# ScalarE and GpSimd preparing the next sub-block, and a transpose moved between two products, in a two-layer kernel's solve stage

## The reference, cut to what matters

```
logits = einsum('bhqd,bhkd->bhqk', q, k) * scale
probs = softmax(logits + causal_mask)
L = eye(s) - tril(probs, -1)
rhs = diagonal(probs)[..., None] * v
A = solve_triangular(L, rhs, lower=True)          # s = 512 rows, one after the other
attn_output @ Wd.T + bd
...
h = gelu(einsum('ecd,edf->ecf', exp_batches, c_fc))
exp_out = einsum('ecf,efd->ecd', h, c_proj)
```

## Time and profile before

| | |
|---|---|
| median of 3 runs | 1405.09 us (1400.81 to 1409.5) |
| the profiled execution's own time | 1403.81 us |
| its span, first to last instruction | 1401.9 us |
| busy in the span: PE, PEld, DVE, ACT, POOL | 981.4, 766.5, 900.0, 466.1, 341.8 us |
| mean granted TensorE clock | 0.818 of full |
| the four `solve_block` stages | about 595 to 713, 808 to 924, 1040 to 1157, 1241 to 1358 us of the span |

### The profile page before, as it was taken

The page is one execution under the profiler, slowest core; times in us unless marked ns, Lnnn a source line. Parts: engine busy times, 40 slices in busy tenths (PEclk is TensorE's granted clock), DMA queues, the critical chain, the costliest instruction groups (busy, mean ns, idle before and its releaser), DMA issues. The chain is left out here.

```text
span 1401.9 us, 29590 instructions
## 1 busy us (share of the span) xinstructions
PE 981.4 (70%) x10762; PEld 766.5 (55%) x10762; DVE 900.0 (64%) x3559; ACT 466.1 (33%) x1066; POOL 341.8 (24%) x390
## 2 busy tenths in 40 slices
PE   5376599970665056877769968769986777986754
PEld 5165499960621034666545657646665655775643
DVE  5656262216789065888768888758878970058857
ACT  1233244424224003311235411235532126941215
POOL 1277154540047170021210021210001230012221
PEclk9788799995579587966889966789977788987877
DMA  9397598836018864410034220044411005411008
GB/s 220 46 209 210 155 249 238 228 95 180 26 50 237 244 151 123 113 28 20 21 97 129 77 61 20 22 110 125 114 46 36 24 21 163 136 45 38 28 22 235
DMA packets 241824, 153.95 MB, mean 110 GB/s; under 512 B 80432, under 2 KB 226096, under 8 KB 241424
## 3 DMA queue, kind: packets, MB, share of 16 engines
q1 hardware_dynamic: 232528, 133.04, 37.0%
q0 software_dynamic: 9152, 19.02, 4.2%
HBM read 96.76 MB, written 55.24 MB: 108 GB/s over the span
## 5 line engine op out<-in xcount | busy, mean ns | idle before, releaser
L1157 DVE TENSOR_REDUCE mx<-banks 128x1 f32<-128x384 f32 (+3 forms) x352 | 203.3, 634 | 72.6 <-PE banks L1088 72.0
L1323 DVE TENSOR_TENSOR prod<-A,Kst_Pn 128x8 f32<-128x8 f32 (+30 forms) x992 | 179.4, 221 | 0.6
L1329 DVE TENSOR_REDUCE A<-prod 128x4 f32<-128x8 f32 (+30 forms) x992 | 174.8, 217 | 0.0
L800 POOL DMA_INDIRECT o_dram<-step_o,step_to x80 | 81.4, 1017 | 309.4 <-ACT step_o L789 297.2
L1137 ACT ACTIVATE Eoff<-banks 128x256 f32<-128x256 f32 (+2 forms) x192 | 114.9, 598 | 102.6 <-PE banks L1073 93.6
L1071 PE MATMUL banks<-Qexp,Kst_Pn 128*128 128x256 bf16 x640 | 115.5, 282 | 44.1 <-DMA Qmax<-q_stack 34.0
L1139 ACT ACTIVATE Ed<-banks 128x256 f32<-128x256 f32 x256 | 98.0, 383 | 111.4 <-PE banks L1073 111.4
L1084 PE MATMUL banks<-masks,identb 128*128 128x128 bf16 (+2 forms) x352 | 90.3, 256 | 59.8 <-DMA Qmax<-q_stack 50.9
L1088 PE MATMUL banks<-Kst_Pn,Qmax 128*128 128x128 bf16 (+3 forms) x512 | 123.3, 313 | 0.0
L756 PE MATMUL banks<-step_xT,step_w 128*128 128x256 f32 x320 | 105.8, 488 | 22.5 <-issue 22.0
L1263 POOL TENSOR_TENSOR A<-A,Kst_Pn 128x256 f32<-128x256 f32 x16 | 19.4, 1213 | 408.0 <-DVE Kst_Pn L1293 408.0
(11 more groups left out here) (197 smaller groups left out, 1816.0 us busy)
## 6 DMA issues: line engine op xcount, KB each, us to landing
Kst_Pn<-k_stack SPq DMA_DIRECT2D x32, 512.0 KB, 4.6
rows_dram<-blank SPq DMA_DIRECT2D x12, 858.0 KB, 12.1
e_w<-in_L_w1T_dram SPq DMA_DIRECT2D x39, 256.0 KB
e_w<-in_L_w2T_dram SPq DMA_DIRECT2D x39, 256.0 KB
Qmax<-q_stack SPq DMA_DIRECT2D x64, 96.0 KB
Qexp<-q_stack SPq DMA_DIRECT2D x64, 96.0 KB
Kst_Pn<-k_stack SPq DMA_DIRECT2D x16, 384.0 KB, 4.5
step_xt<-rows_dram SPq DMA_DIRECT2D x40, 132.0 KB, 2.2
```

The costliest lines, as they stand in the source:

```text
L800: self.nc.gpsimd.indirect_dma_start(self.o_dram, bass.IndirectOffsetOnAxis(self.to[n][:, j:j + 1], 0), self.o[n][:, j, :], None).then_inc( ...
L1157: nc.vector.tensor_reduce(out, logits, AX_X, ALU.max, negate=True).then_inc(max_done, 1)
L1323: nc.vector.tensor_tensor(prod[:, ds, 0:r + 1], A[:, ds, k0:k0 + r + 1], Pn[:, c * SUB + r:c * SUB + r + 1, 0:r + 1].broadcast_to([P, HD / ...
L1329: nc.vector.tensor_reduce(A[:, ds, k0 + r], prod[:, ds, 0:r + 1], AX_X, ALU.add).then_inc(row_done, 1)
```

## The change

VectorE now multiplies only the first sub-block's probabilities. For sub-blocks 1 to 3 ScalarE copies the turned probabilities from PSUM into `Pn` as they are (`keep_probs`), and GpSimd, one sub-block ahead, forms the first term, multiplies `Pn` by `rZ`, multiplies `A` by the diagonal, sets the diagonal to 1 and adds the term (`prepare`). `turn_before(c+1)` moves ahead of sub-block c's recurrence, so that for sub-block 1 it stands before the first recurrence of the block. TensorE's transposes of the next expert tile move between a tile's `up` and its `down`, and ScalarE's copy of them behind the tile's second gelu.

```diff
                 for g in range(per_sub * c, per_sub * (c + 1)):
-                    if g >= 2:
-                        pe.wait_ge(probs_in, g - 1)
+                    if g < 2 * per_sub:
+                        pe.wait_ge(probs_in, g - per_sub + 1)
+                    else:
+                        pe.wait_ge(probs_kept, g - 2 * per_sub + 1)
                     turn_probs(nc, Ed, ident, bank[g % 2], g).then_inc(probs_turned, 1)
...
                 for k in tiles[c]:
-                    steps.turn(pe, k)
+                    if k == tiles[0].start:
+                        steps.turn(pe, k)
                     steps.up(pe, k)
+                    if k + 1 < tiles[-1].stop:
+                        steps.turn(pe, k + 1)
                     steps.down(pe, k)
...
         def _(act):
+            def keep_probs(c):
+                for g in range(per_sub * c, per_sub * (c + 1)):
+                    act.wait_ge(probs_turned, g)
+                    nc.scalar.copy(Pn[:, g * TURN:(g + 1) * TURN, :],
+                                   bank[g % 2][:, 0:TURN * SUB].rearrange("p (q k) -> p q k", k=SUB)).then_inc(probs_kept, 1)
+
             for c in range(NSUB):
+                if c + 1 < NSUB:
+                    keep_probs(c + 1)
                 for k in tiles[c]:
-                    steps.keep_turned(act, k)
+                    if k == tiles[0].start:
+                        steps.keep_turned(act, k)
                     steps.gelu(act, k)
+                    if k + 1 < tiles[-1].stop:
+                        steps.keep_turned(act, k + 1)
                     steps.keep_out(act, k)
...
         def _(pool):
+            own = Chain(pool, own_done)
...
+            def own_term(c):
+                ts = slice(t0 + c * SUB, t0 + (c + 1) * SUB)
+                own(nc.gpsimd.tensor_tensor(A[:, :, ts], A[:, :, ts],
+                                            diagonal(c).rearrange("p (a i) -> p a i", a=1).broadcast_to([P, HD, SUB]), ALU.mult))
+                own(nc.gpsimd.memset(diagonal(c), 1.0))
+
+            def prepare(c):
+                qs, ts = slice(c * SUB, (c + 1) * SUB), slice(t0 + c * SUB, t0 + (c + 1) * SUB)
+                z = rZ[:, qs].rearrange("p (q a) -> p q a", a=1)
+                pool.wait_ge(z_done, c)
+                own(nc.gpsimd.tensor_tensor(term[:, :, :], before[:, :, 0:HD].rearrange("p q d -> p d q"),
+                                            rZ[:, qs].rearrange("p (a q) -> p a q", a=1).broadcast_to([P, HD, SUB]), ALU.mult))
+                pool.wait_ge(probs_kept, per_sub * c)
+                own(nc.gpsimd.tensor_tensor(Pn[:, qs, :], Pn[:, qs, :], z.broadcast_to([P, SUB, SUB]), ALU.mult))
+                own_term(c)
+                own(nc.gpsimd.tensor_tensor(A[:, :, ts], A[:, :, ts], term[:, :, :], ALU.add))
+
+            pool.wait_ge(probs_in, per_sub)
+            own_term(0)
             for c in range(NSUB):
...
+                if c + 1 < NSUB:
+                    prepare(c + 1)
                 for k in tiles[c]:
                     steps.send(pool, k)
...
+            turn_before(0)
+            first_terms()
+            turn_before(1)
             for c in range(NSUB):
-                turn_before(c)
                 if c:
                     keep_rows(c - 1)
-                add_before(c)
-                if c:
+                    if c + 1 < NSUB:
+                        dve.wait_ge(own_done, 2 + 5 * c)
+                        turn_before(c + 1)
                     add_later(c)
-                dve.wait_ge(own_done, 2 * c + 2)
```

More of the change, by code:

```diff
@@ L1191, in solve_block @@
         sb, sem = tensors(nc, ctx)
-        own_done, base_done = sem("own_done"), sem("base_done")
+        own_done, base_done, probs_kept, z_done = sem("own_done"), sem("base_done"), sem("probs_kept"), sem("z_done")
         probs_turned, probs_in = sem("probs_turned"), sem("probs_in")
@@ L1257, in _, with diagonal @@
         def _(pool):
-            for c in range(NSUB):
[L1259 to L1266, removed]
+            own = Chain(pool, own_done)
+            def diagonal(c):
+                first = c * SUB * SUB
+                return Pn.rearrange("p q k -> p (q k)")[:, first:first + (SUB - 1) * (SUB + 1) + 1:SUB + 1]
+            def own_term(c):
[15 more added lines that the diff above has]
+            own_term(0)
+            for c in range(NSUB):
+                if c + 1 < NSUB:
+                    prepare(c + 1)
                 for k in tiles[c]:
@@ L1274, in _, with add_term, first_terms @@
             base = Chain(dve, base_done)
-            def add_term(c, sums):
+            def add_term(c, sums, out, ready):
                 qs = slice(c * SUB, (c + 1) * SUB)
                 ts = slice(t0 + c * SUB, t0 + (c + 1) * SUB)
[L1279 to L1282, removed]
+                base(nc.vector.tensor_tensor(out, sums, rZ[:, qs].rearrange("p (a q) -> p a q", a=1).broadcast_to([P, HD, SUB]), ALU.mult))
+                dve.wait_ge(own_done, ready)
+                base(nc.vector.tensor_tensor(A[:, :, ts], A[:, :, ts], out, ALU.add))
             def turn_before(c):
                 base(nc.vector.transpose(before[:, :, :], RT[:, c, :, :].rearrange("p t q -> p q t")))
-                base(nc.vector.reciprocal(rZ[:, c * SUB:(c + 1) * SUB], before[:, :, HD]))
-            def add_before(c):
-                for g in range(per_sub * c, per_sub * (c + 1)):
+                if c:
+                    nc.vector.reciprocal(rZ[:, c * SUB:(c + 1) * SUB], before[:, :, HD]).then_inc(z_done, 1)
+                else:
+                    base(nc.vector.reciprocal(rZ[:, 0:SUB], before[:, :, HD]))
+            def first_terms():
+                for g in range(per_sub):
                     gs = slice(g * TURN, (g + 1) * TURN)
@@ L1295, in add_before @@
                                             ALU.mult).then_inc(probs_in, 1)
-                add_term(c, before[:, :, 0:HD].rearrange("p q d -> p d q"))
+                add_term(0, before[:, :, 0:HD].rearrange("p q d -> p d q"), later[:, :, :], 2)
             def keep_rows(c):
@@ L1305, in add_later @@
                 base(nc.vector.transpose(later[:, :, :], wide[:, 0:SUB * HD].rearrange("p (t d) -> p d t", d=HD)))
-                add_term(c, later[:, :, :])
+                dve.wait_ge(z_done, c)
+                add_term(c, later[:, :, :], later[:, :, :], 2 + 5 * c)
+            turn_before(0)
+            first_terms()
+            turn_before(1)
             for c in range(NSUB):
-                turn_before(c)
                 if c:
                     keep_rows(c - 1)
-                add_before(c)
-                if c:
+                    if c + 1 < NSUB:
+                        dve.wait_ge(own_done, 2 + 5 * c)
+                        turn_before(c + 1)
                     add_later(c)
-                dve.wait_ge(own_done, 2 * c + 2)
                 k0 = t0 + c * SUB
```

## The result

The changed kernel takes 1414.94 us, the median of 11 runs (1410.99 to 1417.96); the kernel before, over 11 runs in all, 1405.09 (1399.17 to 1409.5). The ratio is 1.0072 with a 95% interval of 1.0055 to 1.0088: slower by 0.7%. The forecast was 1414. The profiled execution took 1415.38, its span 1413.5, which is 11.6 longer than before.

What follows compares the result with a forecast made beforehand. VectorE was taken to set nine of 16 sub-block stretches, TensorE seven. Terms -8.8 + 10.0 + 12.7 + 11.2 - 2.6 - 6.0 - 3.15 - 3.0 gave +10.3 on 1403.81, or 1414 us; range 1385 to 1430.

Steps and rivals of the forecast that it cites:

- block's start: Before each block's first recurrence: the turning for sub-block 1 and a memset wait cost 2.5 a block, +10.0 us.
- lock: GpSimd's SBUF reads hold VectorE's recurrence multiplications: +12.7 us in sub-block 0, +11.2 in sub-block 1; also counted in sub-block 2.
- tiles: Expert tiles: hidden transposes take 1.0 a tile off TensorE's path; sub-block 2 -2.6 and -6.0 us, sub-block 3 -3.15.
- crossings into 1 and 2: From turn_rows to later_sums: the row copy no longer waits behind turning sums, 1.1 at eight crossings, -8.8 us.
- block's end: Earlier GpSimd sends let VectorE's last copy close three of four blocks, 1.0 each, -3.0 us.
- GpSimd beside the recurrence: GpSimd and VectorE take exclusive turns at SBUF: each small operation costs VectorE 0.38 us, the 128x1024 one 2.03.
- second rival: In the recurrence, GpSimd holds VectorE for the whole instruction, 0.69 and 2.76 us: +20.7, 1424 us; chance 0.17.
- first rival: In the recurrence, GpSimd gives way and VectorE doesn't lose: -17.0, 1387 us; chance 0.18.
- third rival: In the tiles, the moved transposes aren't hidden and TensorE's stretches stay as long: +25.1, 1429 us; chance 0.06.
- the 16 stretches: Sub-block spans from later_sums to turn_rows before the change: TensorE taken to set seven, VectorE nine.

Runs made afterwards that it cites:

- e6: Changed kernel with GpSimd's four reading operations per prepared sub-block replaced by memsets that read nothing: 1381.31 us, ratio 0.9844.
- e1: Kernel before with only the expert-tile transposes moved between up and down, and ScalarE's copy behind the gelu: 1379.81 us, ratio 0.9817.
- e10: Changed kernel with useless transposes filling TensorE's waits before turn_rows in sub-blocks 0, 1 and 3, three per recurrence row: 1406.80 us, ratio 1.0001.
- e2: Changed kernel with only the moved transposes taken back, ahead of each tile: 1433.41 us, ratio 1.0201.
- e5: Kernel before with the transposes moved and, at a crossing, the copy of rows ahead of turning the sums: 1375.38 us, ratio 0.9792.
- e8: e5 with useless transposes, four each behind a few late recurrence rows of sub-blocks 0, 1 and 3: 1363.35 us, ratio 0.9702.

## Why the prediction was right, and where two terms were wrong

By its own steps, in us over the four blocks, measured as after less before from the table:

| term | predicted | measured |
|---|---|---|
| sub-block 0 (block's start 10.0 and lock 12.7) | +22.7 | +22.7 |
| sub-block 1 (lock) | +11.2 | +9.4 |
| sub-block 2 (tiles, lock) | -8.6 | -10.0 |
| sub-block 3 (tiles) | -3.15 | -3.2 |
| crossings into 1 and 2 | -8.8 | -1.8 |
| block's end | -3.0 | -7.6 |
| not forecast: `later_sums` +1.7, crossing into 3 -0.1, elsewhere +0.5 | 0 | +2.1 |
| sum | +10.3 | +11.6 |

*GpSimd beside the recurrence* was the step on which the sign hung, and it held: e6 takes the loss away and leaves the rest. The multiplications grew by 34.3 where 35 was forecast. The split was off in both parts and the errors cancelled: a big operation costs 1.40 to 1.63, not 2.03; a small one 0.53, not 0.38. Three guesses were behind that. The big operation takes 1.91 whole, so its hold was not four times the small one's 0.55. VectorE is let go only a little before GpSimd ends: the held pair ends at 642.02 + 1.83 = 643.85 and needs its usual 0.32, so the hold ended near 643.53, 0.13 before GpSimd's 643.66. That is the 0.14 of the last stage's copy (0.61 - 0.47), and it did not grow with the operation. And what VectorE can do meanwhile isn't half a pair of reductions but the whole pair: GpSimd gets in as a pair of multiplications ends (641.75 beside 641.54 + 0.32), and the reductions stand next. So the second rival had the better mechanism, nearly the whole instruction, with a price that no row bore out (2.76). The first rival, that VectorE doesn't lose, would have brought sub-blocks 1 to 19.3; they took 21.72.

*The block's start* came out to the tenth. Timeline of VectorE after, against the earlier trace rows:

```profile
604.20 0.43 DVE L1316 TENSOR_TENSOR A<-A,later 128x256 f32<-128x256 f32 x1 [1.09 <-POOL Kst_Pn L1284]
604.66 2.01 DVE L1319 STREAM_TRANSPOSE before<-RT 128x1024 f32<-128x1024 f32 x1
...
606.97 0.17 DVE L1363 TENSOR_TENSOR prod<-A,Kst_Pn 128x8 f32<-128x8 f32 x2
```

From the block's first `turn_before` (597.98) to the recurrence it is 8.99. Before it was 602.58 - 596.13 = 6.45, so the loss is 2.54 where I took 2.5.

*Tiles.* The move hid as forecast, and the third rival fell. In sub-block 2 TensorE got further than I said: 20.08 in e1, in all blocks alike, where I had taken 22.20 in blocks 1 and 2. It decided nothing, since VectorE's 21.7 ends later there. By VectorE's own price, smaller than forecast, -8.6 became -10.0.

One reading ahead of the forecast was wrong, at a small price. In blocks 1 and 2 TensorE was last in sub-block 1 too, as the missing wait shows (TensorE, kernel before, block 1):

```profile
861.61 1.04 PE L1218 MATMUL banks<-ident_c,A 128*64 128x128 f32 x8
```

So TensorE set nine of the 16 stretches and VectorE seven. In these two blocks sub-block 1 took 19.63 and 19.35 where the others have 19.29 and 19.24, and the crossing behind it 3.06 and 3.34 where the others have 3.43: about 0.4 us of the kernel each.

*The crossing between sub-blocks* failed. I took 1.05 for the row transposes from rows where TensorE had waited 0.69 and 1.52, and did not ask at what clock they would run behind a longer wait, though the same forecast made every wait longer: sub-blocks 0 and 1 that VectorE lengthens, and tiles that end sooner. After 9.13 and 5.71 of waiting they take 1.89 and 1.92 at the lower clock, and ScalarE's and VectorE's copies stand behind them. So the gain of 1.1 became 0.29 and 0.16 a crossing. e10, with the wait filled, has 2.47 and 2.30 on the mean. The forecast's 2.34 was right for transposes at the upper clock.

*The block's end* was mis-sized, the other way. I counted the 1.0 between the ends of GpSimd's last send and VectorE's last copy, as if the stage ended with the later row. Before, at the end of block 1, GpSimd's row ended at 924.03 + 0.96 = 924.99 and SyncE's first load of the next stage came 2.85 later (SyncE's timeline, kernel before):

```profile
927.84 0.33 SPq L1031 DMA_DIRECT2D Kst_Pn<-k_stack  x1
```

After, GpSimd, VectorE and SyncE:

```profile
928.54 1.21 POOL L800 DMA_INDIRECT o_dram<-step_o,step_to  x1 [0.31 <-issue]
...
932.14 1.06 DVE L1338 COPY Apos<-banks 32x512 f32<-32x512 f32 x1 [2.06 <-PE banks L1220]
...
933.95 0.33 SPq L1031 DMA_DIRECT2D Kst_Pn<-k_stack  x1
```

VectorE closes the stage at 933.20, and the load follows 0.75 later. An indirect send as the last thing costs some 2 us more behind its row than VectorE's copy does, and the end of the stage gets rid of that where the sends are early. Block 0 of the kernel before bears this out: there the copy's row ended last, by 0.13, and the load still came 2.84 behind the send (GpSimd, VectorE, SyncE):

```profile
712.33 0.96 POOL L800 DMA_INDIRECT o_dram<-step_o,step_to  x1 [0.30 <-issue]
...
712.36 1.06 DVE L1301 COPY Apos<-banks 32x512 f32<-32x512 f32 x1 [1.19 <-PE banks L1218]
...
716.13 0.36 SPq L1031 DMA_DIRECT2D Kst_Pn<-k_stack  x1
```

So the sends closed all four blocks, not three. From the end of the row transposes, the gap to the next stage fell by 10.6 over the four blocks, and the longer row transposes at the lower clock gave 3.0 of it back. In the kernels with late sends (before and e2) the load comes 2.84 to 3.21 behind the send in all six blocks that another follows; in such blocks of the ten others it comes 0.74 to 1.20 behind the copy. No run changed the sends alone, and what lies between the send's row and the barrier no row shows.

So the step that decides was right in kind, and that the sum was met within 1.3 us is luck, by errors that cancelled: +7.0 at the crossings and +2.1 left open, against -4.6 at the ends and -3.2 in sub-blocks 1 and 2.

## What to carry to other kernels

Before an operation that reads SBUF is moved to GpSimd, ask whether what it will run beside multiplies two SBUF operands on VectorE: here twelve operations of 1.91 and 28 of 0.7 to 0.9 cost the recurrence 34 us, and what VectorE was spared for it had stood in its own waits. Before a duration is carried over to the new schedule, look at how long the engine waited ahead of that row then and now, and on TensorE at the granted clock of the row: a short step behind a longer wait need not be the same row. And try the parts of a change alone: the transposes' move was worth 26 us, hidden under the other part's loss.

## What was not expected of the hardware

Eight row transposes cost 1.05 or 1.89, by the granted clock, and the length of the wait in front does not by itself tell which. In e1 a wait of 3.42 was followed by 1.89 in block 0, and one of 3.36 by 1.05 in block 1 (TensorE of e1):

```profile
623.92 1.89 PE L1218 MATMUL banks<-ident_c,A 128*32 128x128 f32 x8 [3.42 <-DVE A L1335]
...
830.02 1.05 PE L1218 MATMUL banks<-ident_c,A 128*32 128x128 f32 x8 [3.36 <-DVE A L1335]
```

The 4.13 ahead of the last row transposes of block 0, in the changed kernel, was followed by 1.26. The last stretch of a wait that TensorE fills with work of no use can be worth more than its cost where a crossing hangs on it: from e5 to e8 the crossings and ends lost 5.8 us, from the changed kernel to e10 8.5.

In most blocks a stage that ends with GpSimd's indirect send passes its barrier 2.85 behind the send's row, and one that ends with a VectorE copy 0.75 behind the copy's. No row of GpSimd shows the difference; only the next stage's first load does.
